# Contracting two TensorE products over all 128 rows of their tiles instead of 48 and 64

## What is computed

```python
xz = x @ W_in                                   # 256 -> 2 x 512
x_proj, z = jnp.split(xz, 2, axis=-1)
x_conv = silu(causal depthwise conv of x_proj over 4 positions + conv_b)
ssm = x_conv @ W_xproj                          # 1 + 16 + 16 columns
delta = jax.nn.softplus(ssm[..., 0]); Bm = ssm[..., 1:17]; Cm = ssm[..., 17:]
h_mean = jnp.einsum('bld,bln->bdn', x_conv, delta[..., None] * Bm) / L
y = jnp.einsum('bdn,bln->bld', h_mean, Cm) + D * x_conv
x = layernorm(x + (y * silu(z)) @ W_out)
h = silu(fp4(x) @ fp4(w_gate).T) * (fp4(x) @ fp4(w_up).T)      # 256 -> 704
out = layernorm(x + fp4(h) @ fp4(w_down).T)                    # 704 -> 256
```

## Time and profile before

| | |
|---|---|
| median of 3 runs | 1989.16 us (1985.54 to 1989.21) |
| profiled execution, its own time | 1988.75 us |
| its span in the profile | 1987.0 us |
| TensorE busy with matmuls | 97% of the span |
| VectorE, ScalarE, GpSimd busy | 79%, 64%, 55% |

### The profile page before, as it was taken

One profiled execution on the slowest core, in us unless ns is written; L12 is line 12 of the kernel. 1 busy time (PEld: TensorE's weight loads), 2 busy tenths in 40 slices (PEclk: granted clock), 3 DMA queues, 4 the chain that ended last, 5 costly groups with the idle time before them and its releaser, 6 DMA issues. The chain is left out here.

```text
span 1987.0 us, 34279 instructions
## 1 busy us (share of the span) xinstructions
PE 1920.3 (97%) x10180; PEld 1540.1 (78%) x10180; DVE 1578.8 (79%) x3549; ACT 1265.9 (64%) x2617; POOL 1102.5 (55%) x1758
## 2 busy tenths in 40 slices
PE   6898999999999999999999999999999999999996
PEld 5665788888878888888788788888888888777775
DVE  5645788878888888888888888888788887788885
ACT  6776666666666666666666666666666666544443
POOL 3434555556555656655556665565565556555553
PEclk8898999999999999999999999999999999999998
DMA  5234233232322322323223232232323223222210
GB/s 167 96 122 144 91 100 103 89 109 99 102 100 98 99 95 99 109 94 109 96 85 107 99 109 96 99 104 88 109 99 101 100 88 99 69 65 73 72 38 16
DMA packets 120309, 190.60 MB, mean 96 GB/s; under 512 B 15040, under 2 KB 49728, under 8 KB 120128
## 3 DMA queue, kind: packets, MB, share of 16 engines
q1 hardware_dynamic: 120128, 188.42, 28.5%
HBM read 104.48 MB, written 83.89 MB: 95 GB/s over the span
## 5 line engine op out<-in xcount | busy, mean ns | idle before, releaser
L532 PE MATMUL pgu<-wgu_hi,xqT 128*128 128x512 f32 (+1 forms) x1536 | 427.1, 386 | 7.6 <-issue 6.5
L532 PEld LDWEIGHTS pgu<-wgu_hi,xqT 128*128 128x128 f32 x1536 | 278.7, 189 | 72.0 <-issue 9.9
L532 PE MATMUL pd<-wd_hi,hqT 128*128 128x256 f32 (+1 forms) x1536 | 315.9, 297 | 5.2 <-issue 2.1
L532 PEld LDWEIGHTS pd<-wd_hi,hqT 128*128 128x128 f32 (+1 forms) x1536 | 247.7, 190 | 26.6 <-issue 4.8
L1019 DVE SCALAR_TENSOR_TENSOR scratch<-scratch 128x256 f32<-128x256 f32 (+2 forms) x258 | 171.8, 666 | 96.7 <-ACT scratch L898 77.4
L411 POOL TENSOR_SCALAR rs<-ssq 128x1 f32<-128x1 f32 x256 | 72.4, 283 | 310.3 <-issue 297.3
L532 PE MATMUL pgu<-wgu_lo,xqT 128*128 128x512 f32 (+1 forms) x768 | 228.0, 378 | 0.0
L1104 DVE SCALAR_TENSOR_TENSOR acc<-xps,cw,acc 128x512 f32<-128x512 f32 x256 | 200.3, 782 | 30.8 <-POOL acc L450 26.2
L608 PE MATMUL pd<-wout,g 128*128 128x256 f32 x864 | 215.4, 392 | 0.0
L802 ACT ACTIVATE scratch<-scratch,sum 128x256 f32<-128x256 f32 x256 | 130.2, 509 | 123.4 <-DVE scratch L1164 118.4
L472 POOL TENSOR_TENSOR scratch<-hnq,qsh 128x704 f32<-128x704 bf16 x128 | 188.7, 1474 | 0.0
(11 more groups left out here) (140 smaller groups left out, 4489.8 us busy)
## 6 DMA issues: line engine op xcount, KB each, us to landing
sz_hbm<-szs SPq DMA_DIRECT2D x128, 256.0 KB, 2.0
xc_hbm<-xcs SPq DMA_DIRECT2D x128, 256.0 KB, 2.0
early<-xc_hbm SPq DMA_DIRECT2D x128, 256.0 KB, 2.7
early<-sz_hbm SPq DMA_DIRECT2D x128, 256.0 KB, 3.0
xin<-in_x_t_dram SPq DMA_DIRECT2D x32, 512.0 KB, 4.7
xres<-in_L_attn_x_dram SPq DMA_DIRECT2D x128, 128.0 KB, 2.4
out_dram<-scratch SPq DMA_DIRECT2D x128, 128.0 KB, 1.7
early<-in_L_attn_W_in_dram SPq DMA_DIRECT2D x2, 512.0 KB, 4.7
```

The source lines that it names most:

```text
L532: mm = pe.matmul(bank, lhsT, rhs, start=(m == 0), stop=(m == len(pairs) - 1))
```

## The change

`hcat` and `ctr` get 128 rows instead of 48. GpSimd clears both once at the start, rows 48 to 127 stay zero from then on, and the writers still write only rows 0 to 47. The writers wait once for the clearing. The y product then takes 128 rows of both. The last pass of the down product takes all 128 rows of its two operands. Rows 64 to 127 there hold h's rest and the weights' rest, so their product is now added as well. The order of all other instructions is as before.

```diff
-        ctr = sb("ctr", [H3, SPS, ST], F32R)
+        ctr = sb("ctr", [P, SPS, ST], F32R)
...
-        hcat = sb("hcat", [H3, DI], F32R)
+        hcat = sb("hcat", [P, DI], F32R)
...
             pool.memset(nhalf[:, :], -0.5).then_inc(id_ready, 1)
+            pool.memset(ctr[:, :, :].bitcast(F32), 0.0).then_inc(rows_zero, 1)
+            pool.memset(hcat[:, :].bitcast(F32), 0.0).then_inc(rows_zero, 1)
...
                 pairs += [(hqT[:, FC, :], wd_hi[:, FC, :]),
-                          (hqT[0:FR, 2 * FC + 1, :], wd_hi[0:FR, FC, :])]
+                          (hqT[:, 2 * FC + 1, :], wd_hi[:, FC, :])]
                 split_product(pd[:, 0:DM], DM, pairs).then_inc(dn_pe, 1)
...
                         act.wait_ge(ct_pe, g_)
-                        act.activation(ctr[:, (s - 1) % SPS, :], c_bank(g_)[0:H3, :], ACT.Copy).then_inc(ct_ready, 1)
+                        if g_ == 1:
+                            act.wait_ge(rows_zero, 2)
+                        act.activation(ctr[0:H3, (s - 1) % SPS, :], c_bank(g_)[0:H3, :], ACT.Copy).then_inc(ct_ready, 1)
...
                         dve.wait_ge(h_added, g_)
-                        dve.tensor_scalar(hcat[:, :], hacc[:, :], 1.0 / L, None, ALU.mult)\
+                        if b == 1:
+                            dve.wait_ge(rows_zero, 2)
+                        dve.tensor_scalar(hcat[0:H3, :], hacc[:, :], 1.0 / L, None, ALU.mult)\
                             .then_inc(h_link, 1)
```

More of the change, by code:

```diff
@@ L159, in block_kernel @@
         id_zero = sem("id_zero")
+        rows_zero = sem("rows_zero")
         id_ready = sem("id_ready")
```

## The result

The changed kernel takes 1906.41 us (median of 4 runs, 1905.8 to 1906.92) against 1988.8 us before: a ratio of 0.9589, with a 95% interval of 0.9572 to 0.9606. That is 82.4 us less, where 74.3 were forecast. Its profiled execution has a span of 1904.3 us.

What follows compares the result with a forecast made beforehand. TensorE's instruction stream bounds the full stage. Edges 75.5 us, plus 1.5 for groups 5, 6 and 32, less 2.7 of stall, take 74.3 us off 1988.75: called 1914.5 us, range 1904 to 1938.

Steps and rivals of the forecast that it cites:

- The price of the edges: Where 48- or 64-row matmuls stand between 128-row ones: 0.375 us a y product, 0.38 a down product, 0.755 a step.
- The cause: At those places TensorE empties itself and loads weights in the open when the row form changes; chance 0.70.
- Groups 5, 6 and 32: Groups beside the start-up's waits and a TensorE wait for VectorE: 1.5 us saved, from nothing to 6.4.
- The lateness in step 3: VectorE comes 0.29 us late in step 3 as TensorE's work between loses 0.47 us; hidden, barely.
- The stall behind the mean state: Once in four groups TensorE waits 0.455 us for VectorE, six times in groups 7 to 31, 2.7 us.
- if its other waits in between stay: Condition under which VectorE needs 13.83 us from skip to skip around the mean state, against TensorE's 13.27.
- The slack: Between L1202's end and the z half: 0.68 us, of which the change takes 0.285 and leaves 0.395.
- The draining stage: Groups 33 to 38: nothing saved; the gap before the gate product grows from 0.27 to about 0.9 us.
- The clears: GpSimd's clearing at the start costs nothing under a 10.82 us wait; without that cover 1 to 4 us once.
- the second: VectorE becomes the bound in earnest (1935 us), or only one product's edges go (1952 us); chance 0.16.
- The third: Semaphore waits, not rows, keep the y and gate products' loads from being pulled ahead: unchanged at 1989 us; chance 0.08.
- The slower case: TensorE idles on a late VectorE and its clock drops, ending near 2001 us; chance 0.03.

Runs made afterwards that it cites:

- The first and second experiments: Changed kernel with only the y product at 128 rows: 1947.3 us; with only the last down pass at 128 rows: 1946.0 us.

## Why the prediction held

**The bound.** Right. TensorE's stream set the time of the full stage before and sets it now, at a full granted clock; what the edges cost came out of the period nearly one for one.

**The price of the edges.** 0.755 us a step was forecast, 0.782 measured in the group's period. The first and second experiments give 0.377 and 0.393 for the forecast 0.375 and 0.38. The missing 0.01 to 0.03 us a step is no more than what can be lost by adding up distances from rows rounded to 0.01 us. Over 100 steps it is 2.7 us of the 8 us that the forecast is short. The stall came out 1.3 us smaller, and the start-up and the later groups give the rest; all of these erred to the same side.

**The cause.** Right as far as it goes, and now shown rather than argued: the crossing costs, not the matmul. At a crossing the load of the weights begins only as the matmul ahead ends, and without one it begins 0.27 to 0.40 us ahead of that end. That TensorE empties itself there fits these rows, but no record shows the emptying itself. The rule of the Trainium skill in "TensorEngine Tiling (Array Packing)", section Key Properties, that changing the tiling mode drains the engine, agrees with this, and the price is about 0.19 us a crossing for rows, taken as half of an island's 0.38 us. The Trainium skill's rule that only columns count, in "TensorE: Matmul & The Clock Gate", section LDWEIGHTS, holds for a load or a matmul among its like: the load of 48 rows took 0.18 us and that of 128 rows 0.19, the 32-row y product costs what the 48-row one does, and the second 64-row pass 0.10 us. It says nothing of the crossings.

**Groups 5, 6 and 32.** I took 1.5 us out of a range of 0 to 6.4, and with the start-up they gave 5.3. This is the term furthest off. About 1.5 us of it came before the first y product and is scatter. Group 32's period varies as well (50.4 us before, 51.8 with the clears alone, 47.8 now), so how much of the rest is the change's own can't be told.

**VectorE's part.** The lateness in step 3 was forecast as 0.29 us, and it is 0.81 - 0.53 = 0.28, hidden as forecast. The stall behind the mean state was forecast as 0.455 us and is 0.19, and the groups 7 to 31 lose 1.4 us to it and a first, larger one instead of 2.7. The step that failed is "if its other waits in between stay". From skip to skip VectorE took 13.47 us and not 13.83. Most of the difference is its wait for ScalarE, which fell from 0.59 us to 0.32, since ScalarE waited less for TensorE's transposes (0.54 us instead of 1.16) and came earlier too. So VectorE's lateness reached 1.04 - 0.54 = 0.50 us and not 0.85. The slack was a little smaller than my 0.395: the z half starts 0.15 us after L1209 ends, not at once, and the change took 3.68 - 3.46 = 0.22 out of it, not 0.285. That leaves 0.68 - 0.22 - 0.15 = 0.31 us of cover, and 0.50 - 0.31 is the 0.19 of stall. The same assumption made the chain's floor 54.4 us where the experiment without the five passes ran at 53.6.

**The draining stage.** Right: the step stayed at 10.64 us and the saving went into the wait before the gate product. The gap is 0.73 us and not 0.9; why stays open. The stage as a whole was 0.7 us shorter, about what it varies by among the kernels here: 250.1 us before, 249.5 with the clears alone, 249.4 now.

**The clears.** Right. They took 2.3 us, where 1 to 4 were allowed for, under a wait of 10.8, and the version with them alone measures 0.9997.

**The rivals.** Of the second, VectorE does not bind yet, except once in four groups; it would have after another 0.4 us a step or so, by the 1.7 us a group that the version with fewer passes still gained. The third, that loads are held by their semaphores, fell with the row counts: the y product's load waits for the same semaphores with 128, 96, 48 and 32 rows, and only the last two show the edge. The slower case did not come up: the granted clock was 1.00 from 300 to 1000 us.

## What to carry to other kernels

Where TensorE is the bound, look at the distances between the starts of matmuls wherever the number of rows or columns in use changes, and compare them with a place where the same neighbours follow each other without the change. A short contraction set between full ones is cheaper when it is filled up with zero rows, or rows that do no harm, since its own cost goes by columns; filling up to 96 was enough here. Before counting on the whole gain, sum the next engine's chain over one period, and treat a wait for an engine that itself waits for TensorE as something that shrinks.

## What was new about the hardware

- Row forms: 96 rows behave as 128 (55.29 us a group against 55.32), while 32, 48 and 64 rows between 128-row matmuls cost 0.38 to 0.39 us each time. The price did not depend on which of 32 and 48 it was (56.85 and 56.87 us a group).
- At a crossing the weight load begins with its own matmul, 0.07 us ahead of the recorded end of the matmul before it; without one it begins 0.27 to 0.40 us ahead of that end. How the 0.38 us divide between the places around an island is less sure, since the y product's own start moved with its rows (0.31 us behind the transposes before, 0.14 after).
- Columns divide at the same place, between 64 and 96, with a smaller price: an island of eight matmuls with 48 or 64 columns costs 0.29 us, with 96 or 128 none. Float32 transposes with 48 columns showed no price at all (1898.8 us with 128 columns, 1898.4 with 48), and why is open.
